# A recurrent layer's side jobs cut into quarters, one per step, each in place of one of the step's two keep-warm products

## The reference

```python
def step(h, xb_t):
    h = jnp.tanh(h @ A.T + xb_t)
    y = h @ C.T
    return (h, y)
...
xn  = layernorm(x)
xb  = jnp.einsum('bsd,ed->sbe', xn, B)
_, ys = jax.lax.scan(step, h0, xb)
out = jnp.transpose(ys, (1, 0, 2)) + xn
x   = x + layernorm(out) * gamma + beta
x   = x + six_layers(layernorm(x), ...)
```

## Time and profile before

| | |
|---|---|
| runs | 3483.62 us (median of 3), 3481.26 to 3486.61 |
| the profiled execution's own time | 3489.47 us |
| its span | 3487.7 us |
| mean granted TensorE clock | 0.986 |
| TensorE busy (matmul / weight load) | 3341.8 us (96%) / 2160.1 us (62%) |
| VectorE, ScalarE, GpSimd busy | 2797.8 (80%), 2306.6 (66%), 2258.2 us (65%) |
| tanh of the recurrence (L735), 512 | 90.8 us busy |
| keep-warm products (L511), 1024 | 304.0 us busy |

### The profile page before, as it was taken

How to read it: one execution, slowest core, us unless ns; L and a number is a source line. 1 busy time by engine, 2 the same in 40 slices (tenths; PEclk the granted TensorE clock), 3 DMA queues, 4 the chain that set the end, 5 groups by cost and what they waited for, 6 DMA issues and landing times. The chain is left out here.

```text
span 3487.7 us, 101023 instructions
## 1 busy us (share of the span) xinstructions
PE 3341.8 (96%) x42261; PEld 2160.1 (62%) x42261; DVE 2797.8 (80%) x4511; ACT 2306.6 (66%) x4497; POOL 2258.2 (65%) x1364
## 2 busy tenths in 40 slices
PE   8999699999999999999999999999999999999996
PEld 4555366666666666666666666666666666666663
DVE  2333498888898898888898789888898888898983
ACT  2222267777777777777777677776777777777774
POOL 0000267777677777777777677777677776777773
PEclk9999799999999999999999999999999999999999
DMA  2000000100000100001000001000001000000000
GB/s 71 1 1 1 4 11 11 32 11 11 11 13 12 35 11 11 8 17 35 11 11 8 11 17 33 10 11 11 8 17 35 11 11 8 11 17 16 12 11 13
DMA packets 62282, 52.51 MB, mean 15 GB/s; under 512 B 11527, under 2 KB 59397, under 8 KB 61829
## 3 DMA queue, kind: packets, MB, share of 16 engines
q1 hardware_dynamic: 61828, 46.05, 5.1%
HBM read 43.93 MB, written 2.10 MB: 13 GB/s over the span
## 5 line engine op out<-in xcount | busy, mean ns | idle before, releaser
L448 POOL TENSOR_TENSOR cosp<-cosp,rr 128x1024 f32<-128x1024 f32 x384 | 722.6, 1903 | 592.4 <-DVE rr L963 592.3
L458 POOL TENSOR_TENSOR cosp<-cosp,sinp 128x1024 f32<-128x1024 f32 x384 | 902.5, 2370 | 65.9 <-DVE sinp L942 65.9
L543 PE MATMUL ps<-w_qk,xs 128*128 128x512 f32 x1536 | 766.6, 622 | 20.1 <-ACT sq L755 16.5
L644 PEld LDWEIGHTS ps<-px,w_vo 128*128 128x128 f32 x6144 | 701.0, 192 | 57.5 <-ACT px L808 45.7
L644 PE MATMUL ps<-px,w_vo 128*128 128x128 f32 x6144 | 721.4, 276 | 1.9 <-ACT px L808 1.7
L755 ACT ACTIVATE sq<-ps 128x1024 f32<-128x1024 f32 x384 | 392.7, 1023 | 472.9 <-DVE sinp L942 472.9
L939 DVE TENSOR_TENSOR cosp<-ps,tab 128x1024 f32<-128x1024 f32 x384 | 469.3, 1222 | 153.9 <-PE ps L543 152.6
L543 PEld LDWEIGHTS ps<-w_qk,xs 128*128 128x128 f32 x1536 | 264.2, 192 | 387.6 <-issue 378.6
L948 DVE TENSOR_REDUCE ss<-sq 128x16 f32<-128x1024 f32 x384 | 455.3, 1186 | 54.4 <-ACT sq L755 54.3
L942 DVE TENSOR_TENSOR sinp<-ps,tab 128x1024 f32<-128x1024 f32 x384 | 466.4, 1215 | 0.0
L704 PE MATMUL ps<-pT,xtm 32*128 32x512 f32 x3072 | 445.0, 628 | 12.7 <-issue 4.7
(11 more groups left out here) (106 smaller groups left out, 4475.9 us busy)
## 6 DMA issues: line engine op xcount, KB each, us to landing
tab<-in_tab SPq DMA_DIRECT2D x96, 128.0 KB, 2.1
qks<-in_scales SPq DMA_DIRECT2D x96, 128.0 KB, 3.3
w_qk<-in_L_ffn_Wqkv SPq DMA_DIRECT2D x12, 512.0 KB, 6.3
w_v<-in_wv_t SPq DMA_DIRECT2D x6, 512.0 KB, 8.4
w_o<-in_L_ffn_Wo SPq DMA_DIRECT2D x6, 512.0 KB, 9.2
x<-in_L_attn_x SPq DMA_DIRECT2D x16, 128.0 KB, 5.1
out<-w_v SPq DMA_DIRECT2D x16, 128.0 KB, 2.4
w<-in_L_ffn_W SPq DMA_DIRECT2D x6, 341.0 KB
```

The costliest lines, as they stand in the source:

```text
L448: eng.tensor_tensor(v, v, rr[:, B % 2, HEADS * i:HEADS * i + HEADS].unsqueeze(2).to_broadcast([P, HEADS, DH]), ALU.mult).then_inc(rot_read ...
L458: eng.tensor_tensor(cosp[:, A % 2, i, :], cosp[:, A % 2, i, :], sinp[:, i, :], ALU.add).then_inc(rot_added, 1)
L543: t = eng.matmul(ps[:, u, :], xs[:, n % ROUND, :], w_qk[:, n // TILES % 2, i, 512 * u:512 * u + 512], start=True, stop=True)
L644: t = eng.matmul(Y, w_vo[:, i // HP, i % HP, :], px[:, i, :], start=i == 0, stop=i == HEADS - 1)
```

## The change

Each side job is cut into four quarters of 128 columns, one per step, and the chunk's first product becomes a fourth such job. `outputs` runs at t = 3 to 6, `turn_input` at 38 to 41, `turn_xn` now at 46 to 49, and `start_chunk` (new) at 58 to 61 of the chunk before, each quarter between the step's L527 and one keep-warm product instead of two. ScalarE's copies are quarters as well, behind the tanhs of t = 42 to 45 and 50 to 53. The semaphores `hs_turned`, `post_turned`, `ln1_turned`, `xn_out` and `pre_started` count four per chunk; a quarter other than the first waits for nothing of its own on TensorE, and ScalarE's copies wait for all four transposes. The core of the diff:

```diff
-AT_OUTPUT, AT_INPUT, AT_XN = 3, 38, 54
+AT_OUTPUT, AT_INPUT, AT_XN, AT_START = 3, 38, 46, 58
...
-            def turn_xn(c):
-                eng.wait_ge(ln1_step, LN_STEPS * (c + 1))
-                after(eng, xn_out, c)
-                for j in range(TB):
-                    t = eng.transpose(ps[:, 3, P * j:P * j + P], xn_tm[:, c % 2, j, :], ident[:, :])
-                t.then_inc(ln1_turned, 1)
-
-            def outputs(c):
-                eng.wait_ge(hs_done, c + 1)
-                after(eng, post_step, POST_STEPS * c)
-                for j in range(TB):
-                    t = eng.matmul(ps[:, 4, P * j:P * j + P], hs[:, P * j:P * j + P], abcT[:, 2, :], start=True, stop=True)
-                t.then_inc(hs_turned, 1)
-
-            def turn_input(c):
-                eng.wait_ge(post_step, POST_STEPS * (c + 1))
-                after(eng, x_updated, c)
-                for j in range(TB):
-                    t = eng.transpose(ps[:, 5, P * j:P * j + P], lnd[:, j, :], ident[:, :])
-                t.then_inc(post_turned, 1)
+            def turn_xn(c, j):
+                if j == 0:
+                    eng.wait_ge(ln1_step, LN_STEPS * (c + 1))
+                    after(eng, xn_out, TB * c)
+                eng.transpose(ps[:, 3, P * j:P * j + P], xn_tm[:, c % 2, j, :], ident[:, :]).then_inc(ln1_turned, 1)
+
+            def outputs(c, j):
+                if j == 0:
+                    eng.wait_ge(hs_done, c + 1)
+                    after(eng, post_step, POST_STEPS * c)
+                eng.matmul(ps[:, 4, P * j:P * j + P], hs[:, P * j:P * j + P], abcT[:, 2, :], start=True, stop=True).then_inc(hs_turned, 1)
+
+            def turn_input(c, j):
+                if j == 0:
+                    eng.wait_ge(post_step, POST_STEPS * (c + 1))
+                    after(eng, x_updated, c)
+                eng.transpose(ps[:, 5, P * j:P * j + P], lnd[:, j, :], ident[:, :]).then_inc(post_turned, 1)
+
+            def start_chunk(c, i):
+                r, n = c % 2, FW // TB
+                if i == 0:
+                    after(eng, h_done, FW * (c - 1))
+                    eng.wait_ge(xn_out, TB * (c + 1))
+                eng.matmul(ps[:, r, CH // TB * i:CH // TB * i + CH // TB], abcT[:, 1, :],
+                           xn_fm[:, r, :].rearrange("p (b t) -> p t b", b=BATCH)[:, n * i:n * i + n, :],
+                           start=i == 0, stop=False, skip_group_check=True).then_inc(pre_started, 1)
 
             def keep_warm():
                 eng.matmul(ps[:, 7, 0:KEEP].rearrange("p (a n) -> p a n", n=P), ident_bf[:, :],
                            ident_bf[:, :].unsqueeze(1).to_broadcast([P, KEEP // P, P]), start=True, stop=True)
 
-            turn_xn(0)
+            for j in range(TB):
+                turn_xn(0, j)
             eng.wait_ge(abc_out, 1)
             eng.wait_ge(zeroed, 8)
             eng.wait_ge(tables_ready, 2)
+            for i in range(TB):
+                start_chunk(0, i)
             for c in range(NC):
                 r = c % 2
-                after(eng, h_done, FW * c)
-                eng.wait_ge(xn_out, c + 1)
-                eng.matmul(ps[:, r, :], abcT[:, 1, :], xn_fm[:, r, :].rearrange("p (b t) -> p t b", b=BATCH),
-                           start=True, stop=False, skip_group_check=True).then_inc(pre_started, 1)
                 for t in range(FW):
                     after(eng, h_done, FW * c + t)
                     prev = hb[:, r, t - 1, :] if t else hb[:, 1 - r, FW - 1, :]
                     eng.matmul(ps[:, r, BATCH * t:BATCH * t + BATCH], abcT[:, 0, :], prev, start=False, stop=t == FW - 1,
                                skip_group_check=True).then_inc(pre_done, 1)
+                    if c and t - AT_OUTPUT in range(TB):
+                        outputs(c - 1, t - AT_OUTPUT)
+                    elif c and t - AT_INPUT in range(TB):
+                        turn_input(c - 1, t - AT_INPUT)
+                    elif c < NC - 1 and t - AT_XN in range(TB):
+                        turn_xn(c + 1, t - AT_XN)
+                    elif c < NC - 1 and t - AT_START in range(TB):
+                        start_chunk(c + 1, t - AT_START)
+                    else:
+                        keep_warm()
                     keep_warm()
-                    keep_warm()
-                    if t == AT_OUTPUT and c:
-                        outputs(c - 1)
-                    if t == AT_INPUT and c:
-                        turn_input(c - 1)
-                    if t == AT_XN and c < NC - 1:
-                        turn_xn(c + 1)
-            outputs(NC - 1)
+            for j in range(TB):
+                outputs(NC - 1, j)
...
                 if s == 1:
-                    turn_input(NC - 1)
+                    for j in range(TB):
+                        turn_input(NC - 1, j)
...
-            def take_xn(c):
-                eng.wait_ge(ln1_turned, c + 1)
-                after(eng, pre_started, c - 1)
-                eng.copy(xn_fm[:, c % 2, :], ps[:, 3, :]).then_inc(xn_out, 1)
-
-            def take_input(c):
-                eng.wait_ge(post_turned, c + 1)
-                eng.copy(xa[:, :, turn_cols(c)], ps[:, 5, :].rearrange("p (b t) -> p b t", b=BATCH)).then_inc(x_updated, 1)
-
-            take_xn(0)
+            def take_xn(c, j):
+                eng.wait_ge(ln1_turned, TB * (c + 1))
+                if j == 0:
+                    after(eng, pre_started, TB * (c - 1))
+                eng.copy(xn_fm[:, c % 2, P * j:P * j + P], ps[:, 3, P * j:P * j + P]).then_inc(xn_out, 1)
+
+            def take_input(c, j):
+                eng.wait_ge(post_turned, TB * (c + 1))
+                cols = turn_cols(c)
+                ins = eng.copy(xa[:, 2 * j:2 * j + 2, cols], ps[:, 5, P * j:P * j + P].rearrange("p (b t) -> p b t", b=2))
+                if j == TB - 1:
+                    ins.then_inc(x_updated, 1)
+
+            for j in range(TB):
+                take_xn(0, j)
             for c in range(NC):
                 after(eng, hs_done, c - 1)
                 for t in range(FW):
                     eng.wait_ge(pre_done, FW * c + t + 1)
                     eng.activation(hb[:, c % 2, t, :], ps[:, c % 2, BATCH * t:BATCH * t + BATCH], ACT.Tanh).then_inc(h_done, 1)
-                    if t == AT_INPUT and c:
-                        take_input(c - 1)
-                    if t == AT_XN and c < NC - 1:
-                        take_xn(c + 1)
-
+                    if c and t - AT_INPUT - TB in range(TB):
+                        take_input(c - 1, t - AT_INPUT - TB)
+                    if c < NC - 1 and t - AT_XN - TB in range(TB):
+                        take_xn(c + 1, t - AT_XN - TB)
...
                 if s == 1:
-                    take_input(NC - 1)
+                    for j in range(TB):
+                        take_input(NC - 1, j)
```

More of the change, by code:

```diff
@@ L425, in _ @@
                 eng.wait_ge(h_done, FW * c + FW)
-                after(eng, hs_turned, c)
+                after(eng, hs_turned, TB * c)
                 eng.tensor_copy(hs.rearrange("p (b t) -> p b t", b=BATCH), hb[:, c % 2, :, :].rearrange("p t b -> p b t")).then_inc(hs_done, 1)
@@ L886, in normalise @@
             def normalise(c):
-                after(eng, ln1_turned, c - 1)
+                after(eng, ln1_turned, TB * (c - 1))
                 step = Steps(eng, ln1_step, c * LN_STEPS)
@@ L892, in post_sum @@
             def post_sum(c, step):
-                eng.wait_ge(hs_turned, c + 1)
-                after(eng, post_turned, c)
+                eng.wait_ge(hs_turned, TB * (c + 1))
+                after(eng, post_turned, TB * c)
                 step(eng.tensor_tensor(lno, ps[:, 4, :].rearrange("p (j d) -> p j d", j=TB), xn_tm[:, c % 2, :, :], ALU.add))
```

## The result

The changed kernel takes 3455.45 us, the median of 7 runs (3451.31 to 3461.68), against 3479.81 us for the kernel before in as many; the ratio is 0.9924, with a 95% interval of 0.9912 to 0.9936. Three repetitions gave 0.9927, 0.9930 and 0.9929. What follows shows that the steps of the recurrence came out nearly as worked out, and that the remainder comes from a part of the kernel that the prediction held to be fixed.

A forecast was written before the change was run, and what follows sets the result against it. Bound: a 0.655 us ring of tanh and state product, TensorE's queue equally long, side jobs on top. 5.4 + 5.0 + 5.0 + 6.0 - 0.6 = 20.8, said 21: from median 3483.6 to 3462.6 us, range 3455 to 3472.

The forecast's parts named there:

- The start's term: Before the first step, ScalarE makes four copies of 0.26 instead of one of 0.59: +0.3 us, at most +0.45.
- The last chunk's copy: ScalarE's copy in the last chunk, on whose end TensorE waits, is made in quarters too: +0.3 us.
- (a): Outputs in quarters, t=3 to 6 of chunks 1 to 7: 0.22 a quarter, step 0.665, saves 5.4 us.
- (d): Input product in quarters, t=58 to 61 of the chunk before: 0.44 a quarter, step 0.885, saves 6.0 us.
- the ring: Recurrence step: ScalarE's tanh and TensorE's state product alternate; this alone takes 0.655 us, as long as TensorE's queue.
- (b): Turned input, t=38 to 41, copies at t=42 to 45: transposes and copies hidden, cost 0, saves 5.0 us.
- (c): Turned xn at t=46 to 49, copies at t=50 to 53: same as the turned input, saves 5.0 us.
- TensorE's queue has no air: Ordinary recurrence step: L527's passes take 0.23 and two keep-warm products 0.43, filling TensorE up to the next L527.
- (e): Waits in the recurrence stay hidden; the outputs' first quarter waits for GpSimd's states copy, with 1 us to spare.
- The clock rival: Clock falls under the recurrence's transposes: 1.3 us a group, 19 in all, 3481; twice that length 3500; 3% for each.
- A step with transposes would be busier than that: Argument against clock falls: at 1532 TensorE was busy 2.59 of 4.00 us and the clock stayed at 1.00.
- The other rivals: ScalarE's copies not covered, 3477, 3%; input product's quarters fit, 3457, 8%; gain not realised after the recurrence, 3484, 2%.

The follow-up runs named there:

- the experiment: Outputs back in one piece at t = 3 behind both keep-warm products, against the changed kernel; recurrence 347.2 us, ratio 0.9961 to the kernel before.
- the third product: A third keep-warm product in one step of each chunk, against the changed kernel; ratio 0.9936 to the kernel before, the control's 0.9930.
- the kernel with one product: One keep-warm product instead of two in every step of the recurrence, against the changed kernel; recurrence 467.8 us, ratio 1.0296 to the kernel before.
- the shifted one: A third keep-warm product in two steps of each chunk, against the changed kernel; ratios 0.9953 and 0.9958 to the kernel before, mean 3468.9 us.

## Why the prediction was right, and where not

The main claim held: each quarter fits in place of one keep-warm product, steps stay at 0.655, and the recurrence loses what was predicted, 21.9 us measured against 5.4 + 5.0 + 5.0 + 6.0 = 21.4. The start's term, ahead of the first tanh, is 0.24 (13.78 to 14.02) against 0.3, with the four copies in a row taking 0.77 where the sum had 1.04. The last chunk's copy ends 32.07 behind the last tanh instead of 31.87, 0.2 against 0.3. That the steps came out so near is in part luck, as (a) and (d) show. By the steps:

- (a) outputs: 5.5 by the experiment against 5.4, by two errors that cancel. L527 needs 0.14 of the queue and not 0.23, the quarter 0.30 to 0.31 and not 0.22, most of the 0.11 that the bounds allowed for a weight load that nothing hides. The sum, 0.14 + 0.30 + 0.215, is again the ring's 0.655.
- (b), (c) transposes: 10.0 against 10.0. The reason given for ScalarE was right in sum but not in kind: the quarter copy needs 0.16 of a gap, and a whole one would have fitted as well.
- (d) the input product: 6.2 against 6.0. The step is 0.86, not 0.885. Here the quarter was put 0.05 too low (0.44, measured 0.49), and L527 0.09 too high: its 0.23 is the term that the earlier trace rows shows with a wait in it; a queue that is never empty needs 0.14. "TensorE's queue has no air" was therefore wrong by about 0.09 a step, which the third product's price of 0.13 shows again. The ring, not the queue, sets the ordinary step, as the kernel with one product showed at the upper clock level.
- (e) the waits: the states' copy was early by the 1 us worked out. Missed was ScalarE's own second wait at the border, 0.055, six times. It stood in the rows before as well: 2.37 at the first border, 2.43 at the others.
- Rivals. The clock rival's price was fair for one fall of 3.4 us (1.3 us a chunk without the single products; falls of 13.7 us cost up to 4.9) and it didn't happen, but the margin is smaller than the earlier trace rows made it look: without its single products the same group does lose the clock. "A step with transposes would be busier than that" compared spans of busy time, in which a transpose counts like a product. The other rivals did not occur.

The step that failed is the last one of the sum: "All that follows the recurrence waits for its end (ScalarE's first tile inputs stand behind the last tanh), so it moves up as it is." It put the change of that part at nothing, with a scatter of 2.6 us taken from three runs. The part moved up unchanged for its first 30.4 us only. In the two profiled executions it went from 3110.2 to 3094.2 us, 16.0 less, and with the recurrence's 21.7 that makes 3489.47 to 3451.70, where 3468.5 was forecast; and the kernel before alone spreads over 22 us (3470.7 to 3493.1 in 81 executions). Over the executions of both kernels in these comparisons, 81 and 22, the means are 3483.9 and 3457.6 us, 26.3 apart with a standard error of 1.1. The recurrence and its start explain 21.7 (last tanh 377.5 to 355.8), so the layers took 4.6 less. By the granted clock of 74 and 22 of these executions they spent some 88 and 82 us at the lower level; at 0.51 us each that is an estimated 3 of the 4.6, and 10 of the 16.0 of the profiled pair (99.4 and 78.9 us). That something in the change itself made the layers shorter is not needed to explain it, since a small shift alone was followed by a larger difference, in the other direction; it is not ruled out either. Why the clock falls less behind the changed recurrence, and which moment is a good one to begin the layers, stays open; so does why executions of one kernel spread over 18 (22 of the changed one) to 23 us (12 of the shifted one).

## What to carry to other kernels

In a loop bound by a ring of two engines, side jobs are free as long as a step's piece is no longer than what the engine idles or fills with filler; cut them to that size, take the filler out for it, and place the consumer behind a producer that has long finished rather than cutting the consumer. Filler that holds the clock could be swapped here for products of 128 strided fp32 columns, but not for single transposes alone. And a gain of a few us is judged by the stretch in which it arises: the rest of the kernel moved by 5 to 9 us with none of its code changed.

## What was unexpected of the hardware

- A keep-warm rate that hardly raises the clock: with one 512-column product a step the lower level lasted 233 us and came back after 3.4, while with two the upper level was there after one to four steps, and one in groups of four steps (16 steps of 64) didn't lose it.
- A product of fp32 whose moving columns lie 256 B apart took 0.49 a quarter of the input product against 0.30 contiguous. The Trainium skill (SBUF — State Buffer, the note on cachelines under "Door 1: The DMA port swizzle") says that reads that change line at each element pay a penalty; the 0.19 is its size here.
- The same layers, begun 2 us later, took 9 us longer on average (standard error 2), by the profiles most of it in the first 150 us, where the clock's falls differ.
